# Experts stage: VectorE takes the residual, the routing weights, the copy of the turned weights and the statistics in other units of a chunk

## The reference

```python
x = x + 0.5 * ffn(ln(x))            # SwiGLU, int8 weights
x = x + time_mix(ln(x))             # RWKV-style scan
x = x + 0.5 * ffn(ln(x))
x = x + 0.5 * experts(ln(x))        # stage 4 of the kernel
x = x + flow_attention(ln(x))       # stage 5
x = x + 0.5 * experts(ln(x))        # stage 6
```

```python
xn = layernorm(x) * gamma + beta                     # its own norm, on top of ln
abel = gelu(xn @ abel_w + abel_b)
logits = xn @ gate_w + gate_b                        # 8 experts
w = softmax of the two largest logits, 0 for the others
h = gelu(xn @ ew1[e] + eb1[e])                       # 8 experts, 256 hidden each
moe = (sum_e w[e] * (h @ ew2[e] + eb2[e])) @ expm(g0) @ expm(g1) @ expm(g2)
gate = sigmoid([abel, moe] @ gc_w + gc_b)
out = xn_input + abel * (1 - gate) + moe * gate
```

## Time and profile before

| | us |
|---|---|
| median of 3 runs (lowest, highest) | 1096.63 (1096.49, 1097.77) |
| the profiled execution, its own time | 1096.39 |
| its span in the trace | 1094.5 |
| busy: TensorE (matmul) | 891.3 |
| busy: VectorE | 733.3 |
| busy: ScalarE | 663.6 |
| busy: GpSimd | 596.3 |

### The profile page before, as it was taken

One profiled execution on the slowest core, in us unless ns is written; L12 is line 12 of the kernel. 1 busy time (PEld: TensorE's weight loads), 2 busy tenths in 40 slices (PEclk: granted clock), 3 DMA queues, 4 the chain that ended last, 5 costly groups with the idle time before them and its releaser, 6 DMA issues.

```text
span 1094.5 us, 15029 instructions
## 1 busy us (share of the span) xinstructions
PE 891.3 (81%) x3958; PEld 463.1 (42%) x3958; DVE 733.3 (67%) x1656; ACT 663.6 (61%) x1183; POOL 596.3 (54%) x574
## 2 busy tenths in 40 slices
PE   3979967845982898898887689998984799999997
PEld 2864433322431444444443345555542344444443
DVE  4934548986552677777786157777774677777774
ACT  2337759984752777787775254343321778788774
POOL 3523444566456566566667144444447466666664
PEclk9968988776995899999999799999996899999998
DMA  7000000000000000000000000000000000000000
GB/s 200 5 1 1 0 1 1 0 0 1 1 1 0 1 1 1 0 0 0 0 0 1 1 0 1 1 0 1 1 1 0 1 1 10 11 10 10 10 10 20
DMA packets 17932, 8.25 MB, mean 8 GB/s; under 512 B 4169, under 2 KB 17885, under 8 KB 17885
## 3 DMA queue, kind: packets, MB, share of 16 engines
q1 hardware_dynamic: 17884, 7.70, 2.7%
HBM read 5.60 MB, written 2.10 MB: 7 GB/s over the span
## 4 chain that ended last, share of the span: by engine, by line
POOL 33%; issue 30%; PE 16%; DVE 13%; ACT 6%; POOLq 1%; DVEq 0%; ACTq 0%
POOL arena L752 19%; POOL arena L772 4%; POOL arena L719 4%; PE bank L1434 3%; PE bank L1652 3%; PE bank L1436 3%; PE bank L1435 3%; POOL rstd L697 1%; DVE stats L1133 1%; POOL v L705 1%; DVE X L1292 1%; ACT Z L871 1%; PE bank L1659 1%; ACT arena L950 1%; DVE arena L1219 1%
## 5 line engine op out<-in xcount | busy, mean ns | idle before, releaser
L752 POOL TENSOR_TENSOR arena<-arena 128x512 f16<-128x512 f32 x256 | 300.0, 1182 | 181.9 <-ACT arena L950 181.1
L1273 DVE TENSOR_TENSOR arena<-arena,bank 128x512 f32<-128x512 f32 x256 | 172.1, 683 | 93.3 <-ACT arena L955 89.7
L950 ACT ACTIVATE arena<-arena 128x512 f16<-128x512 f32 x256 | 160.5, 627 | 65.4 <-DVE arena L1273 45.2
L955 ACT ACTIVATE arena<-bank,eb 128x512 f32<-128x512 f32 x256 | 173.7, 679 | 35.1 <-PE bank L1436 32.9
L719 POOL TENSOR_TENSOR arena<-arena 128x512 f16<-128x512 f32 x48 | 54.9, 1157 | 84.5 <-ACT arena L884 84.5
L1435 PE MATMUL bank<-arena,ew1hi 128*128 128x512 f16 x256 | 99.0, 387 | 0.0
L1434 PE MATMUL bank<-arena,ew1hi 128*128 128x512 f16 x256 | 99.0, 387 | 0.0
L1436 PE MATMUL bank<-arena,ew1lo 128*128 128x512 f16 x256 | 98.9, 386 | 0.0
L1434 PE MATMUL bank<-arena,ew2hi 128*128 128x512 f16 x256 | 97.6, 381 | 0.8 <-POOL arena L752 0.8
L779 POOL TENSOR_TENSOR arena<-arena 128x512 f32<-128x512 f32 (+1 forms) x24 | 32.6, 1371 | 119.9 <-DVE arena L1398 95.3
L1436 PE MATMUL bank<-arena,ew2lo 128*128 128x512 f16 x256 | 97.5, 381 | 0.0
(11 more groups left out here) (288 smaller groups left out, 1923.5 us busy)
## 6 DMA issues: line engine op xcount, KB each, us to landing
X<-in_L_attn_x_dram SPq DMA_DIRECT2D x8, 256.0 KB, 4.2
out_dram<-X SPq DMA_DIRECT2D x8, 256.0 KB, 2.3
arena<-in_L_ffn_ew_dram SPq DMA_DIRECT2D x1, 1024.0 KB
arena<-in_L_ffn_ew_dram SPq DMA_DIRECT2D x2, 512.0 KB
arena<-in_L_ffn_w_gate_dram SPq DMA_DIRECT2D x1, 192.0 KB, 3.1
arena<-in_L_ffn_w_up_dram SPq DMA_DIRECT2D x1, 192.0 KB, 3.6
arena<-in_L_ffn_w_down_dram SPq DMA_DIRECT2D x1, 192.0 KB, 4.6
arena<-in_L_ffn_gens_dram SPq DMA_DIRECT2D x1, 192.0 KB, 4.6
```

What stands on the lines that cost most here:

```text
L752: pool.tensor_tensor(mo.hlo[:, u % 8, :], mo.hw[:, u % 4, :], mo.hhi[:, u % 8, :], ALU.subtract).then_inc(S.hlo, 1)
L950: A(mo.hhi[:, u % 8, :], mo.hw[:, u % 4, :], ACT.Copy).then_inc(S.hhi, 1)
L955: A(mo.hf[:, u % 4, :], bank[MM1_BANK[u]][:, :], ACT.Gelu, scale=1.0 / WS, bias=eb1[:, u:u + 1]).then_inc(S.gelu, 1)
L1273: TT(mo.hw[:, u % 4, :], mo.hf[:, u % 4, :], bank[3 + (u // EB) % 2][:, :], ALU.mult)\
```

## The change

On VectorE, within a step: the second instruction of the mix, `r`, moves from in front of product 11 to behind it; the routing weights move from behind product 11 to behind product 12; the addition to `X` moves from behind product 13 to behind product 14 and there behind the copy of the turned weights; the statistics move from behind the addition to behind product 15. On TensorE the turn of `r` moves from unit 12 to unit 13. Nothing is added or taken away. `if` blocks are run in the order in which they stand, so in unit 14 the copy comes ahead of the addition.

```diff
@@ VectorE, experts, step, in "for u in range(NU)" @@
                             STT(out=bank[6][:, :], in0=bank[6][:, :], scalar=1.0, in1=mo.dm, op0=ALU.add,
                                 op1=ALU.mult).then_inc(S.m, 1)
+                        if lag and u == 11:
                             dve.wait_ge(S.m, i)
                             STT(out=mo.r, in0=bank[6][:, :], scalar=0.5, in1=mo.ab[:, n, :], op0=ALU.mult,
                                 op1=ALU.add).then_inc(S.r, 1)
...
-                        if lead and u == 11:
+                        if lead and u == 12:
                             dve.wait_ge(S.th, i + 2)
...
-                        if lag and u == 13:
-                            dve.wait_ge(S.rT, i)
-                            dve.wait_ge(S.zadd, i)
-                            if first == 0:
-                                finish_x(i - 1, first, bank[6][:, :], 0.5, S.x, i)
-                            else:
-                                add_to_x(i - 1, first, bank[6][:, :], 0.5, S.x, number)
                         if lead and u == 14:
                             dve.wait_ge(S.wpT, i + 2)
                             dve.tensor_copy(mo.wT[0:2 * E, n, :], bank[7][0:2 * E, 0:CH // 2].bitcast(F16))\
                                .then_inc(S.wT, 1)
+                        if lag and u == 14:
+                            dve.wait_ge(S.rT, i)
+                            dve.wait_ge(S.zadd, i)
+                            add_to_x(i - 1, first, bank[6][:, :], 0.5, S.x, number)
+                        if lag and u == NU - 1 and number < 6:
+                            wait_apart(dve, S.x, i)
+                            tile_stats(i - 1 - first)
@@ TensorE, experts, step @@
-                        if lag and u == 12:
+                        if lag and u == 13:
                             pe.wait_ge(S.r, i)
```

## The result

The changed kernel takes 1099.40 us (median of 20 runs, 1098.02 to 1102.44), the kernel before 1097.36 us (20 runs, 1095.42 to 1100.78): a ratio of 1.0022 with a 95% interval of 1.0013 to 1.0030, so 2.4 us slower (1.4 to 3.3; the plain difference of the two medians is 2.0). The forecast was 1102.2 us, 5.6 us above the 1096.63 measured then: it had the right side and the waits it named, and was more than twice too large.

What follows compares the result with a forecast made beforehand. TensorE, the busiest engine (81% of the span), was taken as the bound, through its waits. The profiled 1096.39 us plus 5.7, with the median 0.24 above that execution, gave 1102.2 us; range 1094.5 to 1105.

Steps and rivals of the forecast that it cites:

- The statistics: Stage 4 steps: moved behind product 15, the statistics cost nothing; gain up to 0.91 us a step.
- The mix: TensorE's turn of `r`, now in unit 13: its 0.25 us wait goes and no new one comes.
- The price of the routing weights: VectorE's L1324 to L1328 wait for GpSimd's subtractions; weights ready 1.25 us later, a new TensorE wait of 0.9 us.
- Copy before the addition: VectorE's residual after the copy ends about +8.03, so TensorE's abhi products wait 0.6 us, a second new wait.
- The head of the next step: ScalarE's abel gelu starts 0.2 us after L1599 with no pause to catch up: 0.2 us, bound nothing.
- The sum: Six full steps per stage: 0.0 us each in stage 4, +0.9 in stage 6; +0.2 near stage 5; +5.7 in all.
- The small instructions: Rival at L1324 to L1328: they meet subtraction 11 alone, weights ready about +4.7; 1087 us, chance 0.15.
- the clock: Rival: after TensorE's three stops the clock falls in each step, 1.5 us each, twelve times; 1120 us, chance 0.05.
- half stalls: Rival: waits and handovers at their low ends in both stages, twelve steps near nothing; 1094.5 to 1098.5 us, chance 0.13.

## Why the prediction was right in kind and wrong in size

**The statistics** were covered behind product 15, and of the 0.91 us a step that the prediction gave them at most in stage 4 they bring 0.88 when they move alone (29.22 against 30.10). Right.

**The mix.** Its wait goes, no new one comes at the turn: right. Done alone it brings nothing (30.13 and 29.22), for the time is spent at the next wait.

**The price of the routing weights.** L1324 and L1325 of the prediction were to take until +4.25 and +5.41 behind unit 12, the weights to be ready at +5.87; measured +4.20, +5.32 and +5.76 (468.71, 469.83 and 470.27 less 464.51), the wait 0.88 us where 0.9 was said. Right.

**Copy before the addition.** This is the step of the prediction that failed, in size and not in kind: the second new wait was put at 0.6 us and measured 0.42. The addition was to end at +8.03 and did at +7.97, and the abel product to start at about +8.2; it started at +8.03, for I took a handover of 0.17 us and this one costs 0.06. So unit 0 came at +8.68 instead of +8.85.

**The head of the next step**: 473.19 to 494.46, the next unit 12, is 21.27 us, against 21.05 in stage 4 before. The 0.2 us were right.

**The sum.** The prediction's step was 0.15 us too long in each stage (30.1 against 29.95), so five full steps of stage 4 came to -0.75 instead of 0 and five of stage 6 to +3.80 instead of +4.5. The piece behind them was to cost 0.2 us in stage 4 and 0.9 in stage 6; it cost -0.46 and +0.77. Together 5.6 us forecast and 3.4 measured in these pieces. (The prediction's own terms, 1096.39, 5.7 and 0.24, add up to 1102.3 and not 1102.2; nothing hangs on that.) Of a sum made of a gain and losses of nearly its size, the difference of 0.15 us repeated twelve times is 1.8 us, a third. In stage 4 the steps behind the last full one gain too, to which the prediction gave nothing: with the statistics alone that piece takes 40.99 us instead of 42.20, 1.21 less where a full step gains 0.88.

The remaining 1 us down to the measured 2.4 us (1.4 to 3.3) stays open. It has the size of what the first chunk of stage 4 was shorter by in all three traces of the changed kernel, 0.65 to 1.0 us, which is in no term of the sum. But the kernel with the addition first warns against reading it so: its traces are 1.2 us longer than the first one of the kernel before from the first full step of each stage on, its first chunk is no shorter, and yet its medians lie 1.4 and 1.7 us below the kernel before. The executions of it that were traced took 1098.02 and 1096.82 us, 2.2 and 0.9 above those medians, so a trace need not show what the median run did.

That the short first chunk is TensorE's clock is shown. In stage 4 the early rise and the clock behind the stop go together: in five of the 14 traces (the changed kernel 3 of 3, the two kernels with the weights in the pause) TensorE reached unit 12 within 21.35 to 21.73 us of the first turn and the clock stayed at 1.00 behind the stop; in the other nine it took 22.06 to 22.08 us, and the clock fell to 0.60 or 0.63. Among the nine are both of the kernel with the addition first, whose instructions up to there are those of the changed one; each of the three kernels traced more than once did the same every time. In stage 6 the clock fell behind the stop in all 14 traces (0.60 to 0.65), the three of the changed kernel among them. What decides it isn't settled: something in each program that no edit here names, or chance, would both fit. And what the clock did in the 20 timed runs was not measured.

**Which part costs.** The prediction booked 0.9 us to the weights and 0.6 to the addition, which is where TensorE's waits stand. The experiments turn that around. From the statistics alone (29.2) the late addition adds 1.20 us a step, the mix nothing (30.43 with it), and the weights' move takes 0.48 off again. With the addition early the same move of the weights costs 0.40 us in stage 4 and 0.17 in stage 6, so an edit has no price of its own apart from the others. A wait shows where a delay surfaces in one order of the list, not what the edit in question costs; the weights' own wait was bought with product 12 and gelu 14 sooner.

**The rivals.** The small instructions don't slip through; the clock doesn't fall in full steps (1.00 with stops of 1.57, 0.88 and 0.42 us); half stalls was nearest in size, 2.4 us against 1.9 at its upper edge (1098.5 less 1096.63), and the handover at the abel product was at its low end as it says; but the wait at the turn of the weights was as long as forecast, 0.88 us.

## What to carry to other kernels

Where four engines pass units on, measure an edit by the change of one full step, the distance between two like instructions in the steady part (it repeated within 0.03 us here), and not by the span of one trace. Then hold the sum against the timed runs, for a traced execution lay up to 3.3 us from its kernel's median (1108.67 against 1105.39 us with the addition late). Look for what fills an idle gap in front of a product whose input is late: work taken out of such a gap comes back later (here the addition of 0.67 us, moved from ahead of product 14 to behind the copy, cost 1.20 us a step). Put small VectorE instructions from SBUF to SBUF into GpSimd's pauses; four of 0.19 us cost 2.5 us between subtractions and 0.74 us in the pause.

## What the runs showed of the hardware

Of four small VectorE instructions issued while GpSimd subtracts back to back, two were caught and paid the rest of a subtraction, and two passed in a gap or behind the last one. They took 0.19, 1.03, 0.18 and 1.09 us in one order (the weights alone) and 1.03, 1.08, 0.18 and 0.19 in another (the changed kernel), so the moment of arrival decides which is caught, not its kind (tensor-tensor, tensor-scalar and scalar-tensor-tensor were all caught once).

The same instructions on TensorE met different clocks. With the engine idle at 0.50 (1.2 GHz) before, and then busy, the rise to 1.00 (2.4 GHz) came some 2.6 us sooner in one trace than in another. In stage 4 a stop of 2.5 us was followed by a mean of 0.60 or 0.63 over the next 4.3 us in nine traces and by 1.00 in five, the five in which the clock had risen early; in stage 6 it fell in all 14. The fall cost 0.30 us up to the next unit 12 where the clock fell (29.66 against 29.36). Stops of 1.57, 0.88 and 0.42 us within a full step left it at 1.00.
